# A graph network block on one core: the inverse transform of its convolution as 64-row matmuls on two halves of TensorE's array

## The chip, the cores and the metric

One Trainium2 chip, one NeuronCore of it. The metric is the time of one execution on the device, in microseconds (us). An execution is given by the median of the runs that were timed; a profiled execution has a time of its own, and beside it a span, from its first instruction to its last.

## What is computed

64 graphs of 256 nodes with 256 channels go through two layers, each fed with relu(layernorm(x)) and added to x. Layer 0 is a normalised graph convolution. Layer 1 takes three things from its input h:

```python
xc = transpose(h)                       # channels x nodes
c  = relu(bn(conv1d(xc, w1, 0)))        # 1 tap
c  = bn(conv1d(c, w2, 8))               # 17 taps along the 256 nodes, 256 -> 256 channels
x_conv = transpose(relu(c + xc))
A = exp(-dist(h));  x_nmp = A @ relu(h @ w_msg.T + b_msg)
gi = concat(x_conv, x_nmp) @ w_ih.T + b_ih
gh = h @ w_hh.T + b_hh                  # then the three gates of a GRU cell
out = x + (1 - z) * tanh(gi_n + r * gh_n) + z * h
```

## The kernel before, in words

The convolution with 17 taps is computed by overlap and add in the frequency domain. Each graph's 256 nodes are cut into four tiles of 64, each is transformed with length NT = 80 (80 real rows of spectrum), multiplied bin by bin with the transformed filter, and transformed back. The inverse transform of one graph takes 4 x 80 = 320 rows of spectrum, for 256 output channels, to 256 nodes, tiles overlapping by 16 nodes.

The program has three stages. In the first (0 to 690 us of the profile) a software pipeline goes over the 64 graphs: layer 0, the norms, the one-tap convolution, the messages and the forward transform. In the second (690 to 906 us) TensorE multiplies the spectra of all graphs with the filter, bin by bin, and the products go to a DRAM tensor, `y_d`. In the third (906 to 1789 us) a loop goes over 32 pairs of graphs: inverse transforms, then the matmuls of the gates (`gate`, all recorded on L113, in `multiply`). Most matmuls of this kernel split each number in a high and a low part of type fp32r and take three products; the inverse transform is one plain fp32 matmul per product, and an fp32 matmul leaves two records of LDWEIGHTS and two of MATMUL in the trace.

Around the change:

- `load_y` (L917 to L924), on SyncE's queue, brings the 320 rows of graph b to one of three buffers, `yt`: one DMA for the rows 0 to 127 and 192 to 319 (pieces of 1 KB), one for the rows 128 to 191 on partitions 0 to 63. It waits until the transform of graph b - 3 is done. `y_d` is padded by 64 rows for the first DMA's reading pattern.
- Partitions 64 to 127 of the third block are set to zero once, by three memsets on GpSimd (L1474), so that this block too is a matmul over 128 rows; `idft` waits for them (`yz`).
- `idft` (L1007 to L1022), on TensorE, does per graph and half of the output channels (o) three matmuls: stationary operand 128 rows x 128 channels of `yt`, moving operand 136, 136 and 144 columns of the table `gt`, accumulated in PSUM. Both halves lie in one bank, 4 + b % 2.
- `branch_sum` (L1024, VectorE) adds bias and h to the bank, `branch_scalar` (L1053, ScalarE) and `branch_lo` (L1042, VectorE) make the high and low parts `xcx`, which the gates of the next pair read. 
- The order on TensorE is written out in the loop over the pairs: gates of the first half of the channels (36 matmuls), `idft(b + 2)`, gates of the second half (36 matmuls) with `idft(b + 3)` ahead of the last 18 of them. Only the first pair differs: `idft(0)` and `idft(1)` stand together inside its first gates. There the gate HN of the second half (`hn_bank`, bank 6) is computed ahead of its turn; otherwise HN is in bank 0.

The borders of the blocks are in this line:

```python
BLOCKS = ((0, 128, 0, 136), (192, 320, 120, 256), (128, 192, 56, 200))   # rows from, to; nodes from, to
```

Of the kernel before, what the change touches and what calls it, by code (L numbers as in the profile page):

```python
# [8 lines left out]
F32 = mybir.dt.float32  # L9
F32R = mybir.dt.float32r  # L10
ACT = mybir.ActivationFunctionType
# [3 lines left out]
NT = 80  # L15
# [26 lines left out]

BLOCKS = ((0, 128, 0, 136), (192, 320, 120, 256), (128, 192, 56, 200))


def idft_table():

    g = np.zeros((4 * NT, 4 * TILE + 16))  # L50
    for j in range(4):
        g[j * NT:j * NT + NT, j * TILE:j * TILE + NT] = spectrum_rows(np.arange(NT) - 8, True).T
    out = np.zeros((128, sum(end - first for _, _, first, end in BLOCKS)))
    at = 0
    for top, bottom, first, end in BLOCKS:
        out[0:bottom - top, at:at + end - first] = g[top:bottom, first + 8:end + 8]
        at += end - first
    return out.astype(np.float32)


def tap_table():
# [58 lines left out]
ldx0 ldx1 lda0 lda1 lat0 lat1 st0 ag0a ag0 deg0 degm rs0 dd sd sbias hd ah agg aghi aglo  # L120
out0 u x2 sx20 sx21 st1 ag1a ag1 rs1 n1b xn xnt xt sxt xxhi xxlo s uvf uvh uv cm0 cm1 tcm0 tcm1 h1 mshi mslo
dist af am axhi axlo nmp nm snm dft0 dft1 xe0 xe1 sxa0 sxa1 sxb0 sxb1
unit yz wev wevd lxh0 lxh1 xsum xhi xlo wsum wpart whi0 whi wlo frq com mt ye sy0 sy1 sy2 sy3
lwg0 lwg1 lwg2 lwg3 lwg4 lwg5 wghi wg ly0 ly1 ly2 lxn0 lxn1 lnm0 lnm1 nmhi nmlov nmlop xnhi xnlov xnlop
idf xct xchi xclo ghn gr gin gz gn tr v w nn tz dl e oo lx20 lx21 ot osb so0 so1
""".split()
# [2 lines left out]
def gnn_kernel(nc, x, adj, adjt, w0t, w1mt, wset, wgt, w2r, bc, cols, ftab, gtab, ttab, eye, out):  # L129
    NB = x.shape[0]  # L130
# [12 lines left out]
    xh_d = nc.dram_tensor("xh_d", (128, 2, NF // 2, NG, 64), F32, kind="Internal").ap()  # L143
    xn_d = nc.dram_tensor("xn_d", (NP, 128, 2, 2, 256), F32, kind="Internal").ap()
    x2_v = x2_d.rearrange(blocked, n=2, i=32, h=2, k=32)
    y_all = nc.dram_tensor("y_d", (NB * 4 * NT + 64, 256), F32, kind="Internal").ap()
    y_d = y_all[0:NB * 4 * NT].rearrange("(b r) o -> b r o", b=NB)
    nm_d = nc.dram_tensor("nm_d", (NB, 128, 512), F32, kind="Internal").ap()

    with ExitStack() as ctx:  # L150
        S = {n: ctx.enter_context(nc.semaphore(n)) for n in NAMES}
        P = [ctx.enter_context(nc.psum_tensor(f"P{i}", [128, 512], F32)) for i in range(8)]
# [2 lines left out]
        ident = keep("ident", [128, 128])  # L155
        col = keep("col", [128, 32])
        cold = keep("cold", [128, 24])
        gt = keep("gt", [128, 416])
        bse, low_u, low_v = col[:, 28:29], col[:, 29:30], col[:, 30:31]
        b2, hrz, hn_b, n_b = cold[:, 6:8], cold[:, 8:12], cold[:, 12:14], col[:, 20:22]  # L160
        tt_w = keep("tt_w", [119, 567])
# [69 lines left out]
        yo = [p2(f"yo{i}", [128, 512]) for i in range(4)]  # L231

        xnx.append(p3.hl("xnx1", [128, 2, 512]))
        yt = [p3(f"yt{i}", [128, 3, 256]) for i in range(3)]
        nmx = [p3.hl(f"nmx{i}", [128, 2, 512]) for i in range(2)]
        xct = [p3(f"xct{i}", [128, 2, 256]) for i in range(2)]
        xcx = [p3.hl(f"xcx{i}", [128, 2, 2, 256]) for i in range(2)]
# [679 lines left out]
        def load_y(e, b):  # L917
            e.wait_ge(S["frq"], 2 * NF)
            e.wait_ge(S["idf"], b - 2)
            for n in (b // 32, b // 32 + 2):  # L920
                e.wait_ge(S[f"sy{n}"], 16 * (2 * NF // 4))
            e.e.dma_start(yt[b % 3][:, 0:2, :], y_all[4 * NT * b:4 * NT * b + 384].rearrange(
                "(k p) o -> p k o", p=192)[0:128]).then_inc(S[f"ly{b % 3}"], 16)
            e.e.dma_start(yt[b % 3][0:64, 2, :], y_d[b][128:192]).then_inc(S[f"ly{b % 3}"], 16)  # L924

        def load_pair(e, p):
            e.wait_ge(S["whi"], 30)
# [73 lines left out]
            e.e.tensor_tensor(o[1][:, :, :], xnf[p % 2][:, :, :, :].rearrange("p c i t -> p c (i t)"),  # L1001
                              o[0][:, :, :], ALU.subtract).then_inc(done, 1)

        def idft_bank(b):
            return 4 + b % 2

        def idft(e, b):  # L1007
            k = idft_bank(b)
            e.wait_ge(S[f"ly{b % 3}"], 2 * loaded(b, 3))
            e.wait_ge(S["gt_in"], 16)  # L1010
            e.wait_ge(S["yz"], 1)
            e.wait_ge(S["xct"], b - 1)
            y = yt[b % 3]
            for o in range(2):


                g = 0
                for j, (_, _, first, end) in enumerate(BLOCKS):
                    t = e.e.matmul(P[k][:, o * 256 + first:o * 256 + end], y[:, j, o * 128:o * 128 + 128],  # L1019
                                   gt[:, g:g + end - first], start=o == 0 and j == 0, stop=j == 2, skip_group_check=True)  # L1020
                    g += end - first
            t.then_inc(S["idf"], 1)  # L1022

        def branch_sum(e, b):  # L1024
            p, n = b // 2, b % 2
            t = xct[b % 2]
            e.wait_ge(S["idf"], b + 1)
            e.wait_ge(S[f"lxn{p % 2}"], loaded(p, 2))
            e.wait_ge(S["xclo"], b - 1)
            e.wait_ge(S["xchi"], b - 1)  # L1030
            for c in range(2):
                d = e.e.scalar_tensor_tensor(out=t[:, c, :], in0=P[idft_bank(b)][:, c * 256:c * 256 + 256],
                                             scalar=b2[:, c:c + 1], in1=xnf[p % 2][:, c, n, :],
                                             op0=ALU.add, op1=ALU.add)
            d.then_inc(S["xct"], 1)
# [19 lines left out]

        HN, R, IN, Z = 0, 1, 2, 3
        LAST_Z = (Z, HN)

        def hn_bank(n):

            return 6 if n == 1 else HN

        def gate(e, p, o, k, n, blocks, first, last, at=0, end=512):
            xc = [h[:, :, :, :].rearrange("p c i t -> p c (i t)") for h in xcx[p % 2]]
# [6 lines left out]
        def gates_tensor(e, p, o, middle, late):  # L1071
            n = 2 * p + o
            e.wait_ge(S["xnhi"], p + 1)
            e.wait_ge(S["xnlov"], 1)
            e.wait_ge(S["xnlop"], p)
            e.wait_ge(S["wg"], 2)
            e.wait_ge(S["ye"], 2 * NF - 1)
            e.wait_ge(S["gn"], n)
            if n != 1:
                gate(e, p, o, HN, 2, [4, 5], True, True).then_inc(S["ghn"], 1)  # L1080
            e.wait_ge(S["ye"], 2 * NF)
            e.wait_ge(S["tr"], n)
            gate(e, p, o, R, 0, [4, 5], True, False)
            if n == 0:
                gate(e, p, o, Z, 1, [4, 5], True, False)
            e.wait_ge(S["wg"], 4)
            e.wait_ge(S["nmhi"], 2 * p + 2)
            e.wait_ge(S["nmlov"], 2)
            e.wait_ge(S["nmlop"], 2 * p)
            gate(e, p, o, R, 0, [2, 3], False, False)  # L1090
            if n == 0:
                gate(e, p, o, Z, 1, [2, 3], False, False)
                middle()
                gate(e, p, o, IN, 2, [2, 3], True, False)
                gate(e, p, 1, hn_bank(1), 2, [4, 5], True, True).then_inc(S["ghn"], 1)
            e.wait_ge(S["wg"], 6)
            e.wait_ge(S["xchi"], 2 * p + 2)
            e.wait_ge(S["xclo"], 2 * p + 2)
            gate(e, p, o, R, 0, [0, 1], False, True).then_inc(S["gr"], 1)
            if n == 0:  # L1100
                gate(e, p, o, IN, 2, [0, 1], False, True).then_inc(S["gin"], 1)
                gate(e, p, o, Z, 1, [0, 1], False, True).then_inc(S["gz"], 1)
                return
            e.wait_ge(S["w"], n)
            gate(e, p, o, IN, 2, [2, 3, 0, 1], True, True).then_inc(S["gin"], 1)
            late()
            e.wait_ge(S["tz"], n)
            if n == 2 * NP - 1:

                e.wait_ge(S["gn"], 2 * NP)  # L1110
                for i, k in enumerate(LAST_Z):
                    gate(e, p, o, k, 1, [4, 5, 2, 3, 0, 1], True, True, 256 * i, 256 * i + 256).then_inc(S["gz"], 1)
                return
            gate(e, p, o, Z, 1, [4, 5, 2, 3, 0, 1], True, True).then_inc(S["gz"], 1)

        def gates_scalar(e, p, o, middle, late):
            n = 2 * p + o
            e.wait_ge(S["ghn"], n + 1)
            e.wait_ge(S["nn"], n)
            e.e.activation(gn[:, :], P[hn_bank(n)][:, :], ACT.Identity, scale=0.5, bias=hn_b[:, o:o + 1]).then_inc(S["gn"], 1)  # L1120
            middle()
            e.wait_ge(S["gr"], n + 1)
            e.wait_ge(S["e"], n)
            e.e.activation(tr[:, :], P[R][:, :], ACT.Tanh, scale=0.5, bias=hrz[:, o:o + 1]).then_inc(S["tr"], 1)  # L1124
            e.wait_ge(S["w"], n + 1)
            e.wait_ge(S["oo"], n)
            e.e.activation(nn[:, :], gn[:, :], ACT.Tanh, bias=n_b[:, o:o + 1]).then_inc(S["nn"], 1)  # L1127
            late()
            if n == 2 * NP - 1:
                e.wait_ge(S["oo"], n)  # L1130
                for i, k in enumerate(LAST_Z):
                    e.wait_ge(S["gz"], n + 1 + i)
                    e.e.activation(tz[:, 256 * i:256 * i + 256], P[k][:, 0:256], ACT.Tanh, scale=0.5,
                                   bias=hrz[:, 2 + o:3 + o]).then_inc(S["tz"], 1)
                return
            e.wait_ge(S["gz"], n + 1)
            e.wait_ge(S["oo"], n)
            e.e.activation(tz[:, :], P[Z][:, :], ACT.Tanh, scale=0.5, bias=hrz[:, 2 + o:3 + o]).then_inc(S["tz"], 1)  # L1138
# [303 lines left out]
        def _(gpsimd):  # L1442
# [27 lines left out]
                spectra_lo(e, f)  # L1470
            e.wait_ge(S["xlo"], NF)
            e.wait_ge(S["frq"], 2 * NF)
            for t in yt:
                d = gpsimd.memset(t[64:128, 2, :], 0.0)  # L1474
            d.then_inc(S["yz"], 1)
            e.wait_ge(S["yz"], 1)
            for p in range(NP - 1):
                split_xn_lo(e, p + 1, S["xnlop"])
                split_nm_lo(e, 2 * p + 2, S["nmlop"])
# [86 lines left out]
```

## Time and profile before

| | us |
|---|---|
| median of 3 runs (1788.72 to 1789.57) | 1789.55 |
| the profiled execution | 1790.36 |
| its span | 1788.6 |
| PE, matmuls, busy | 1774.4 (99%) |
| PEld, weight loads, busy | 1574.9 (88%) |
| DVE (VectorE) busy | 1212.5 (68%) |
| ACT (ScalarE) busy | 997.3 (56%) |
| POOL (GpSimd) busy | 830.7 (46%) |

PE is TensorE with its matmuls and PEld the same engine with its weight loads, which overlap the matmuls. Matmuls are pipelined and their recorded ends are modelled, so the duration of one record is longer than the step from one to the next; the chain of waits gives the steps.

### The profile page before, as it was taken

What the parts mean: (1) busy time and instruction counts of PE and PEld (TensorE: products, weight loads), DVE (VectorE), ACT (ScalarE), POOL (GpSimd) and SP (SyncE); (2) the same over time, 40 slices, a digit from 0 to 9 for tenths busy, and PEclk for the clock granted to TensorE, in tenths of its full rate; (3) what the DMA queues carried; (4) which work ended last, traced back from release to release, by engine and by line L of the source; (5) the groups of instructions that cost most, each with busy time, mean ns of one, the idle gap of its engine ahead of it and who ended that gap; (6) DMA issues with size and microseconds to landing.
All of it is one profiled execution on the core that took longest, in us unless ns stands there. A gap on an engine that the chain in (4) does not pass through costs nothing.

```text
span 1788.6 us, 29955 instructions
## 1 busy us (share of the span) xinstructions
PE 1774.4 (99%) x10266; PEld 1574.9 (88%) x10266; DVE 1212.5 (68%) x2318; ACT 997.3 (56%) x1787; POOL 830.7 (46%) x991
## 2 busy tenths in 40 slices
PE   8999999999999999999999999999999999999998
PEld 7999999999999999999988888888888888888887
DVE  8999999999999847665664454554554544545545
ACT  5888888888888876665743233233332332332322
POOL 5788888887777627655722122221221221212211
PEclk9999999999999999999999999999999999999999
DMA  6566666676656554544762534534435345344342
GB/s 214 179 201 210 206 207 209 201 214 191 209 184 202 144 163 148 179 161 171 245 189 73 123 79 108 116 78 116 93 97 120 79 107 116 81 115 101 91 111 42
DMA packets 511381, 262.56 MB, mean 147 GB/s; under 512 B 366215, under 2 KB 474119, under 8 KB 511230
## 3 DMA queue, kind: packets, MB, share of 16 engines
q1 hardware_dynamic: 510686, 260.58, 52.3%
q8 instruction: 83, 1.36, 0.3%
q14 instruction: 68, 0.56, 0.1%
q10 hardware_dynamic: 544, 0.07, 0.0%
HBM read 151.51 MB, written 109.05 MB: 146 GB/s over the span
## 4 chain that ended last, share of the span: by engine, by line
PE 97%; issue 1%; POOL 1%; DVE 0%; ACT 0%; DMA 0%; SPq 0%; POOLq 0%; ACTq 0%; DVEq 0%
PE P L113 72%; PE P L615 6%; PE P L1019 5%; PE P L874 4%; PE P L644 4%; PE P L706 3%; PE P L663 1%; PE P L624 1%; PE P L1488 1%; DMA tt_w<-in_ttab 0%; POOL axl L578 0%; POOL af L575 0%; ACT xn L354 0%; DVE wh0l L837 0%; DVE x L473 0%
## 5 line engine op out<-in xcount | busy, mean ns | idle before, releaser
L1001 POOL TENSOR_TENSOR xnx1l<-xnf,xnx1h 128x1024 fp32r<-128x1024 f32 x16 | 44.2, 2761 | 336.2 <-ACT xnx1h L994 336.2
L1001 POOL TENSOR_TENSOR xnx0l<-xnf,xnx0h 128x1024 fp32r<-128x1024 f32 x15 | 41.6, 2774 | 317.1 <-ACT xnx0h L994 317.1
L1124 ACT ACTIVATE tr<-P,cold 128x512 f32<-128x512 f32 x64 | 44.2, 690 | 192.3 <-PE P L113 192.3
L1127 ACT ACTIVATE nn<-gn,col 128x512 f32<-128x512 f32 x64 | 46.4, 724 | 182.3 <-DVE gn L1148 182.3
L1157 DVE SCALAR_TENSOR_TENSOR tz<-tz,tr 128x512 f32<-128x512 f32 x63 | 43.6, 692 | 142.5 <-ACT tz L1138 142.5
L1138 ACT ACTIVATE tz<-P,cold 128x512 f32<-128x512 f32 x63 | 43.4, 688 | 156.8 <-PE P L113 156.8
L1144 DVE SCALAR_TENSOR_TENSOR gn<-tr,gn 128x512 f32<-128x512 f32 x64 | 45.0, 703 | 125.9 <-ACT tr L1124 125.9
L575 POOL TENSOR_TENSOR af<-af,at 128x512 f32<-128x512 f32 x64 | 110.1, 1720 | 42.8 <-ACT af L366 40.5
L578 POOL TENSOR_TENSOR axl<-af,axh 128x512 fp32r<-128x512 f32 x64 | 101.2, 1582 | 55.6 <-ACT axh L384 55.6
L615 PE MATMUL P<-ah,hd 128*128 128x256 f32 x512 | 121.4, 380 | 0.0
L113 PE MATMUL P<-w1mh,xxh 128*128 128x512 f32 x256 | 107.9, 422 | 0.0
L1019 PEld LDWEIGHTS P<-gt,yt 128*128 128x128 f32 x768 | 98.9, 190 | 4.9
L615 PEld LDWEIGHTS P<-ah,hd 128*128 128x128 f32 x512 | 93.2, 191 | 10.0
L113 PE MATMUL P<-w1mh,xxl 128*128 128x512 f32 x256 | 101.2, 395 | 0.0
L113 PE MATMUL P<-w1ml,xxh 128*128 128x512 f32 x256 | 101.1, 395 | 0.0
L1019 PE MATMUL P<-gt,yt 128*128 128x136 f32 (+1 forms) x768 | 100.8, 281 | 0.0
L498 DVE SCALAR_TENSOR_TENSOR x<-x,x 128x512 f32<-128x512 f32 x64 | 99.8, 1559 | 0.1
L899 DVE TENSOR_TENSOR yo<-P,mt 128x512 f32<-128x512 f32 x78 | 53.5, 686 | 66.5 <-PE P L113 66.5
L1148 DVE TENSOR_TENSOR gn<-gn,P 128x512 f32<-128x512 f32 x64 | 44.0, 688 | 66.9 <-PE P L113 66.9
L706 PE MATMUL P<-tt_w,taps 119*128 119x140 f32 (+1 forms) x592 | 80.8, 283 | 0.0
L113 PE MATMUL P<-w0h,agh 128*128 128x256 f32 x256 | 77.5, 303 | 3.2 <-DVE w0l L463 2.1
L726 ACT COPY wf<-P 128x420 f32<-128x420 f32 (+1 forms) x94 | 46.8, 512 | 60.1 <-PE P L706 59.9
(215 smaller groups left out, 6423.0 us busy)
## 6 DMA issues: line engine op xcount, KB each, us to landing
xh_d<-xst SPq DMA_DIRECT2D x64, 320.0 KB, 4.6
y_d<-yo SPq DMA_DIRECT2D x80, 256.0 KB, 2.2
xl<-xh_d SPq DMA_DIRECT2D x36, 512.0 KB, 4.5
x<-in_x SPq DMA_DIRECT2D x64, 256.0 KB, 2.7
a<-in_adj SPq DMA_DIRECT2D x64, 256.0 KB, 3.1
at<-in_adjt SPq DMA_DIRECT2D x64, 256.0 KB, 3.9
x_d<-x SPq DMA_DIRECT2D x64, 256.0 KB, 4.2
xn_d<-xt SPq DMA_DIRECT2D x64, 256.0 KB, 4.0
```

The source lines that it names most:

```text
L113: done = e.matmul(o, l, r, start=start, stop=stop, skip_group_check=True)
L498: e.e.scalar_tensor_tensor(out=o[:, :, :], in0=o[:, :, :], scalar=0.0, in1=xs[b % 5][:, :, :], op0=ALU.max, op1=ALU.add).then_inc(S["x2"], 1)
L575: e.e.tensor_tensor(af[:, :], af[:, :], at[b % 7][:, :], ALU.mult).then_inc(S["am"], 1)
L578: e.e.tensor_tensor(ax[1][:, :], af[:, :], ax[0][:, :], ALU.subtract).then_inc(S["axlo"], 1)
L615: t = e.e.matmul(P[AG][:, f * 256:f * 256 + 256], hd[b % 2][:, m, f * 128:f * 128 + 128], ah[b % 2][:, m * 256:m * 256 + 256], start=m == ...
L644: t = e.e.matmul(P[k][:, n * 2 * NT:n * 2 * NT + 2 * NT], h1[b % 2][:, n, c * 128:c * 128 + 128], ft[:, :], start=True, stop=True, skip_gr ...
L706: t = e.e.matmul(P[k][:, m * 140:m * 140 + 140], taps[0:n_rows, j0 + m, c * 128:c * 128 + 128], tt_w[0:n_rows, part * 140:part * 140 + 140 ...
L726: e.e.copy(dst, src).then_inc(S["wev"], 1)
L874: t = e.e.matmul(common(chunk)[:, 0:256], xsum[f % 3][:, c, 128 * chunk:128 * chunk + 128], wsum[f % 3][:, c, :], start=c == 0, stop=c == ...
L899: e.e.tensor_tensor(yo[n % 4][:, :].rearrange("p (q o) -> p q o", q=2), main(chunk)[:, :].rearrange("p (q o) -> p q o", q=2), mt[chunk][:, ...
L1001: e.e.tensor_tensor(o[1][:, :, :], xnf[p % 2][:, :, :, :].rearrange("p c i t -> p c (i t)"), o[0][:, :, :], ALU.subtract).then_inc(done, 1)
L1019: t = e.e.matmul(P[k][:, o * 256 + first:o * 256 + end], y[:, j, o * 128:o * 128 + 128], gt[:, g:g + end - first], start=o == 0 and j == 0 ...
```

## The change

The 320 rows of a graph are cut into five blocks of 64 rows. Each block reaches the nodes of REACHED. The half o of the output channels uses partitions 64 o to 64 o + 63 for its spectrum and for a copy of the table, and accumulates in a bank of its own, 4 + 2 (b % 2) + o. The matmuls of the two halves alternate. The table grows from 416 to 560 columns, the buffers `yt` from 3 x 256 to 5 x 128 numbers per partition, the memsets and the padding go, and HN always uses bank 0, so that the early HN of the first pair waits for ScalarE to have read the bank (`gn`).

```diff
-BLOCKS = ((0, 128, 0, 136), (192, 320, 120, 256), (128, 192, 56, 200))
+REACHED = ((0, 72), (0, 136), (56, 200), (120, 256), (184, 256))
+GT_COLUMNS = sum(end - first for first, end in REACHED)
...
+    out = np.concatenate([g[64 * q:64 * q + 64, first + 8:end + 8] for q, (first, end) in enumerate(REACHED)], axis=1)
+    return np.concatenate([out, out]).astype(np.float32)
...
-        yt = [p3(f"yt{i}", [128, 3, 256]) for i in range(3)]
+        yt = [p3(f"yt{i}", [128, 5, 128]) for i in range(3)]
...
-            e.e.dma_start(yt[b % 3][:, 0:2, :], y_all[4 * NT * b:4 * NT * b + 384].rearrange(
-                "(k p) o -> p k o", p=192)[0:128]).then_inc(S[f"ly{b % 3}"], 16)
-            e.e.dma_start(yt[b % 3][0:64, 2, :], y_d[b][128:192]).then_inc(S[f"ly{b % 3}"], 16)
+            for o in range(2):
+                e.e.dma_start(yt[b % 3][64 * o:64 * o + 64, :, :], y_d[b].rearrange("(q p) o -> p q o", p=64)[
+                    :, :, 128 * o:128 * o + 128]).then_inc(S[f"ly{b % 3}"], 16)
...
-        def idft_bank(b):
-            return 4 + b % 2
+        def idft_bank(b, o):
+            return 4 + 2 * (b % 2) + o
...
-            e.wait_ge(S["yz"], 1)
...
-            for o in range(2):
-                g = 0
-                for j, (_, _, first, end) in enumerate(BLOCKS):
-                    t = e.e.matmul(P[k][:, o * 256 + first:o * 256 + end], y[:, j, o * 128:o * 128 + 128],
-                                   gt[:, g:g + end - first], start=o == 0 and j == 0, stop=j == 2, skip_group_check=True)
-                    g += end - first
+            g = 0
+            for q, (first, end) in enumerate(REACHED):
+                for o in range(2):
+                    rows = slice(64 * o, 64 * o + 64)
+                    t = e.e.matmul(P[idft_bank(b, o)][:, first:end], y[rows, q, :], gt[rows, g:g + end - first],
+                                   start=q == 0, stop=q == 4, skip_group_check=True)
+                g += end - first
...
-                gate(e, p, 1, hn_bank(1), 2, [4, 5], True, True).then_inc(S["ghn"], 1)
+                e.wait_ge(S["gn"], 1)
+                gate(e, p, 1, HN, 2, [4, 5], True, True).then_inc(S["ghn"], 1)
...
-            for t in yt:
-                d = gpsimd.memset(t[64:128, 2, :], 0.0)
-            d.then_inc(S["yz"], 1)
-            e.wait_ge(S["yz"], 1)
...
-    nc = bacc.Bacc("TRN2", target_bir_lowering=False, num_devices=1)
+    nc = bacc.Bacc("TRN2", target_bir_lowering=False, num_devices=1, dynamic_dma_scratch_size=8192)
```

## Rows read from the trace of the kernel before

**Rows 1.** The stages: busy time of each engine in three stretches
```profile
core 0: us, PE busy (x) PEld busy (x) DVE busy (x) ACT busy (x) POOL busy (x), PEclk, DMA share, GB/s
0.00:690.00 690.00, 681.08 (x4456) 626.51 (x4457) 635.01 (x1509) 582.15 (x1142) 503.17 (x825) 1.00 0.63 193
690.00:906.00 216.00, 216.00 (x1571) 208.08 (x1570) 134.84 (x159) 135.37 (x228) 135.41 (x71) 1.00 0.56 191
906.00:1788.60 882.60, 877.35 (x4242) 740.33 (x4240) 442.66 (x651) 279.81 (x418) 192.09 (x96) 1.00 0.44 100
```

**Rows 2.** The page's chain that ended last, by line
```profile
PE P L113 72%; PE P L615 6%; PE P L1019 5%; PE P L874 4%; PE P L644 4%; PE P L706 3%; PE P L663 1%; PE P L624 1%; PE P L1488 1%; DMA tt_w<-in_ttab 0%; POOL axl L578 0%; POOL af L575 0%; ACT xn L354 0%; DVE wh0l L837 0%; DVE x L473 0%
```

**Rows 3.** The chain of waits, 1160 to 1210 us: start, us, what
```profile
1167.79 1.42 PE P L1019 x12
1169.21 8.21 PE P L113 x36
1177.42 1.42 PE P L1019 x12
1178.83 16.37 PE P L113 x72
```

**Rows 4.** Groups of instructions by line and form: busy us, mean ns
```profile
L1019 PE MATMUL P<-gt,yt 128*128 128x136 f32 x512 | 80.1, 279 | 0.0
...
L1019 PE MATMUL P<-gt,yt 128*128 128x144 f32 x256 | 52.4, 286 | 0.0
...
L1019 PEld LDWEIGHTS P<-gt,yt 128*128 128x128 f32 x768 | 98.9, 190 | 4.9
```

**Rows 5.** The timeline around one transform: start, us, what
```profile
1204.44 0.39 PE L113 MATMUL P<-xcx0h,wgl 128*128 128x512 f32 x1
1204.44 1.59 PEld L1019 LDWEIGHTS P<-gt,yt 128*128 128x128 f32 x12
1204.67 1.58 PE L1019 MATMUL P<-gt,yt 128*128 128x136 f32 x12
...
1205.99 0.49 PE L113 MATMUL P<-xnx0h,wgh 128*128 128x512 f32 x1
```

**Rows 6.** Four transposes on PE's timeline, and their group by form
```profile
505.23 0.60 PE L663 MATMUL P<-ident,xn 128*128 128x128 f32 x4
...
L663 PE MATMUL P<-ident,xn 128*128 128x128 f32 x256 | 38.4, 273 | 0.9 <-ACT xn L354 0.9
```

**Rows 7.** PE's timeline, first stage: a product over 96 rows between others
```profile
499.97 0.60 PE L615 MATMUL P<-ah,hd 128*128 128x256 f32 x2
500.22 0.59 PE L624 MATMUL P<-uv 96*128 96x256 f32 x2
500.64 0.28 PE L113 MATMUL P<-xxh,wseh 128*128 128x256 f32 x1
```

**Rows 8.** Groups by form, second stage: the filter's transform
```profile
L706 PE MATMUL P<-tt_w,taps 119*128 119x140 f32 x372 | 52.3, 283 | 0.0
...
L706 PE MATMUL P<-tt_w,taps 68*128 68x140 f32 x12 | 2.4, 283 | 0.0
```

**Rows 9.** Timelines of ACT, DVE and PE in the first pair
```profile
908.46 0.68 ACT L1120 ACTIVATE gn<-P,cold 128x512 f32<-128x512 f32 x1
...
916.43 1.48 DVE L1042 SCALAR_TENSOR_TENSOR xcx0l<-xct,xcx0h 128x512 fp32r<-128x512 f32 x2
...
916.81 0.39 PE L113 MATMUL P<-xnx0h,wgh 128*128 128x512 f32 x1
...
918.18 0.40 PE L113 MATMUL P<-xcx0h,wgh 128*128 128x512 f32 x1
```

**Rows 10.** The instructions on the tile yt, and their landings
```profile
L922 SPq DMA_DIRECT2D yt<-y_d x64: 371/502/1418, 907.1 to 1732.5; - x64
L924 SPq DMA_DIRECT2D yt<-y_d x64: 472/483/1473, 907.5 to 1733.0; - x64
L1474 POOL MEMSET yt<- x3: 311/311/313, 906.0 to 906.5; 64x256 f32 x3
...
DMA to landing us min/median/max: 2.4/3.7/6.0
```

**Rows 11.** Timeline of SyncE's queue, and the chain, around one load
```profile
922.20 0.59 SPq L922 DMA_DIRECT2D yt<-y_d x1
...
948.48 1.42 PE P L1019 x12
```

More of the change, by code:

```diff
@@ L52, in idft_table @@
         g[j * NT:j * NT + NT, j * TILE:j * TILE + NT] = spectrum_rows(np.arange(NT) - 8, True).T
[L53 to L58, printed above, removed]
+    out = np.concatenate([g[64 * q:64 * q + 64, first + 8:end + 8] for q, (first, end) in enumerate(REACHED)], axis=1)
+    return np.concatenate([out, out]).astype(np.float32)
 def tap_table():
@@ L122 @@
 dist af am axhi axlo nmp nm snm dft0 dft1 xe0 xe1 sxa0 sxa1 sxb0 sxb1
-unit yz wev wevd lxh0 lxh1 xsum xhi xlo wsum wpart whi0 whi wlo frq com mt ye sy0 sy1 sy2 sy3
+unit wev wevd lxh0 lxh1 xsum xhi xlo wsum wpart whi0 whi wlo frq com mt ye sy0 sy1 sy2 sy3
 lwg0 lwg1 lwg2 lwg3 lwg4 lwg5 wghi wg ly0 ly1 ly2 lxn0 lxn1 lnm0 lnm1 nmhi nmlov nmlop xnhi xnlov xnlop
@@ L145, in gnn_kernel @@
     x2_v = x2_d.rearrange(blocked, n=2, i=32, h=2, k=32)
-    y_all = nc.dram_tensor("y_d", (NB * 4 * NT + 64, 256), F32, kind="Internal").ap()
-    y_d = y_all[0:NB * 4 * NT].rearrange("(b r) o -> b r o", b=NB)
+    y_d = nc.dram_tensor("y_d", (NB, 4 * NT, 256), F32, kind="Internal").ap()
     nm_d = nc.dram_tensor("nm_d", (NB, 128, 512), F32, kind="Internal").ap()
@@ L157, in gnn_kernel @@
         cold = keep("cold", [128, 24])
-        gt = keep("gt", [128, 416])
+        gt = keep("gt", [128, GT_COLUMNS])
         bse, low_u, low_v = col[:, 28:29], col[:, 29:30], col[:, 30:31]
@@ L1002, in split_xn_lo @@
                               o[0][:, :, :], ALU.subtract).then_inc(done, 1)
-        def idft_bank(b):
-            return 4 + b % 2
+        def idft_bank(b, o):
+            return 4 + 2 * (b % 2) + o
         def idft(e, b):
-            k = idft_bank(b)
             e.wait_ge(S[f"ly{b % 3}"], 2 * loaded(b, 3))
             e.wait_ge(S["gt_in"], 16)
-            e.wait_ge(S["yz"], 1)
             e.wait_ge(S["xct"], b - 1)
             y = yt[b % 3]
-            for o in range(2):
-                g = 0
-                for j, (_, _, first, end) in enumerate(BLOCKS):
-                    t = e.e.matmul(P[k][:, o * 256 + first:o * 256 + end], y[:, j, o * 128:o * 128 + 128],
-                                   gt[:, g:g + end - first], start=o == 0 and j == 0, stop=j == 2, skip_group_check=True)
-                    g += end - first
+            g = 0
[5 more added lines that the diff above has]
+                g += end - first
             t.then_inc(S["idf"], 1)
@@ L1031, in branch_sum @@
             for c in range(2):
-                d = e.e.scalar_tensor_tensor(out=t[:, c, :], in0=P[idft_bank(b)][:, c * 256:c * 256 + 256],
+                d = e.e.scalar_tensor_tensor(out=t[:, c, :], in0=P[idft_bank(b, c)][:, 0:256],
                                              scalar=b2[:, c:c + 1], in1=xnf[p % 2][:, c, n, :],
@@ L1057, in gnn_kernel @@
         LAST_Z = (Z, HN)
-        def hn_bank(n):
-            return 6 if n == 1 else HN
         def gate(e, p, o, k, n, blocks, first, last, at=0, end=512):
@@ L1119, in gates_scalar @@
             e.wait_ge(S["nn"], n)
-            e.e.activation(gn[:, :], P[hn_bank(n)][:, :], ACT.Identity, scale=0.5, bias=hn_b[:, o:o + 1]).then_inc(S["gn"], 1)
+            e.e.activation(gn[:, :], P[HN][:, :], ACT.Identity, scale=0.5, bias=hn_b[:, o:o + 1]).then_inc(S["gn"], 1)
             middle()
```

## The prediction

> **What bounds the kernel now.** I read the stages first: TensorE is busy for 877 of the 883 us of the third stage, at a granted clock of 1.00 (the 2.4 GHz level), while VectorE is busy for half of it and ScalarE for a third [rows 1]. The chain that ended last says the same: nearly all of it is PE, and 5% of the span is L1019, the inverse transform [rows 2]. The chain of waits in one pair gives its price: one transform takes 1.42 us, and the next gates begin where it ends, with no piece between [rows 3]. So what the change does to the 64 transforms on TensorE goes to the end one for one: 64 x 1.42 = 90.9 us, which agrees with the 5%. All else counts only if it comes late.
>
> Inside a transform there are 12 records (6 fp32 matmuls, two records each), of 136 and 144 columns [rows 4]. 2 x (136 + 136 + 144) x 2 records = 1664 columns in 1.42 us is 0.85 ns per column. The weight loads last 0.19 us each, yet 12 of them lie side by side in 1.59 us and start ahead of their matmuls [rows 4, 5]: they are hidden now. TensorE is bound by columns here, and the change cuts the columns but adds records: 5 blocks x 2 halves x 2 records = 20 loads and 20 matmuls, of 72, 136, 144, 136 and 72 columns: 560 x 2 x 2 = 2240 columns. Only if the two halves of the array stream at the same time does this fall to the worth of 1120.
>
> **The sum, part by part.**
>
> *Columns and loads.* A record of 72 columns would stream in 72 x 0.85 = 0.061 us, but its next weights must come too. What is the shortest step that a load allows? Nothing in the trace has fewer than 128 columns on both sides; four transposes of 128 columns take 0.60 us from the first's start to the last's end, and one record lasts 0.273 [rows 6]: (0.60 - 0.273) / 3 = 0.109 per step. 128 columns at 0.85 are also 0.109, so this row bounds the floor from above and does not show it: 0.109 at most, 0.061 at least. I take 0.109, because it is the nearest row with a load per record, and keep 0.061 as the other end.
>
> *Overlap.* Matmuls run in program order. In the new order (two records of half 0, two of half 1, and again) the second record of half 0 can run beside the first of half 1, the second of half 1 beside the first of the next block. That gives 11 slots for 20 records: with 0.109 for the 4 slots that hold 72 columns alone, 0.116 for the 4 whose longer record has 136, 0.123 for the 3 with 144, 0.436 + 0.464 + 0.369 = 1.27 us. With 0.061 in the 4 short slots it is 1.08. Against 1.42 that is -0.15 (to -0.34) per transform, 64 x = **-9.6 us** (to -21.8). No row of this trace shows two matmuls at once, so the other end is none of it: 8 x 0.109 + 8 x 0.116 + 4 x 0.123 = 2.29 us, +55.7 us in all.
>
> *Switching the array's division.* Each visit to the transform now goes from instructions over all rows to instructions over half of them, and back: 63 visits (graphs 0 and 1 share one), 126 switches. Lower bound 0: a product over 96 rows between 128-row ones ends 0.24 us after its predecessor for two matmuls (500.57 to 500.81), no more than the 0.12 steps around it [rows 7]; a group over 68 rows has the duration of one over 119 [rows 8]; and the change from fp32 to fp32r behind a transform costs nothing either (1206.25 to 1206.48, the usual 0.23) [rows 5]. A gain is excluded, since a step can't end before its columns are in. But none of these rows divides the array in two that work apart. If the array must be empty before it is divided anew, a switch costs the tail that is hidden now: the 12 records reach over 1.58 us while TensorE moves on by 1.42 [rows 3, 5], so 0.16. If the first load behind the switch can't be hidden either, 0.16 + 0.19 = 0.35 [rows 4]. I take 0.16: nearer to what a division must do than the rows with 0, which change only how many rows of one array are filled. 126 x 0.16 = **+20.2 us** (0 to +44).
>
> The Trainium skill speaks against the change here: "TensorEngine Tiling (Array Packing)", Key Properties, states that changing the tiling mode drains TensorE, while tiles within a mode run loads and matmuls in parallel. It gives no price: by it the sum is that of the emptied array, 1800, and not that of the rows with 0, 1780, and the overlap is real. No run here shows either half yet.
>
> *The wait for `gn` in the first pair.* ScalarE ends `gn` at 909.14; the early HN gate begins at 916.81 [rows 9]. 7.7 us of slack, cost nothing; it would take a ScalarE that is late by that much. Behind the waiting HN stand the last gates of the pair, which wait for `xcx`'s low parts (916.43 + 1.48 = 917.91) and begin at 918.18 [rows 9]. This chain hangs on the end of the second transform and moves with it; once, at most some tenths of a us.
>
> *Loads of the spectrum.* Two DMAs per graph before and after, the same 320 KB, but 640 pieces of 512 B in place of 320 of 1 KB. Issue on SyncE's queue is some 0.5 us each, landing 3.7 us in the median [rows 10]. The load issued at 922.20 is for the transform at 948.48 [rows 11]: 26 us. Even a landing twice as long is hidden, and DMA is at 0.44 of its time [rows 1]. Cost nothing; if the cover went, it would be a wait of TensorE ahead of L1019.
>
> *Memsets, table, banks, DMA scratch.* Three memsets (0.31 us each on GpSimd, at 906 [rows 10]) go: they end 6 us before the first transform. The table is loaded once, in the first stage. VectorE reads two banks in place of one, with as many instructions. No DMA is issued from GpSimd. All nothing.
>
> **Sum**: -9.6 + 20.2 = +10.6 us. Against the profiled execution's own 1790.36 that is 1801.0; the median of the runs stands 0.8 below it, so the forecast for the median is 1800.
>
> **Rivals.** (B) *Overlap without a price of switching*, the other side: the rows with 96 and 68 rows and the type change all switch for nothing [rows 5, 7, 8]. Then -9.6 to -21.8 us: **1768 to 1780**. It decides as soon as a switch costs less than 0.076 us (9.6 / 126). Against it: those rows keep one array.
> (C) *The matmuls overlap, the loads don't.* 20 loads one behind the other at 0.109 are 2.18 us, +0.76, +48.6 us: **1838**, with switches 1858. For it: the 12 loads of a transform start one per step, never two together [rows 5]. Against it: each of them fills all rows, so they could not do otherwise.
> (D) *The change doesn't do what it says*: the halves run one after the other, 2.29 us, +55.7: **1845**, with switches 1865. For it: no row shows two matmuls at once. By the Trainium skill's section neither C nor D should happen.
>
> **Chances.** Forecast (overlap, switches cost 0.08 to 0.35, -1.6 to +34.5 us, 1788 to 1824) 0.41; B 0.34; C 0.11; D 0.14. The range has to leave out at most 0.2: from B's low end, 1768, to just over C's, 1842; D and the dear half of C are outside. The likeliest case's own range is 1788 to 1824. 0.2% (3.6 us) is about what a measurement of this kernel can tell from no change. Faster: B and a little of the forecast's low end, 0.36; same 0.09; slower 0.55.
>
> **What would show it.** In the chain of waits after, one transform (x20) takes 1.4 to 1.6 us if the forecast holds, with two records of L1019 starting within some 10 ns of each other, steps of 0.11 to 0.12 per pair, and a stop of about 0.16 us ahead of the first record and behind the last. B: 1.1 to 1.27 us and gates that follow at once. C: pairs of matmuls start together but only each 0.22 us. D: 20 starts, each 0.11 or more apart, 2.3 us. It would be wrong altogether if TensorE waited for `yt`, or if the clock fell from 1.00 in the third stage as half of the array idles; then the gates' step of 0.23 would grow as well.

## The result, and the profile after

The changed kernel takes 1794.45 us (median of 9 runs, 1794.24 to 1795.23) against 1789.55 us: ratio 1.0029, 95% interval 1.0018 to 1.0039. It is slower by 4.9 us. The forecast was 10.6 us slower: the side was right, the size twice too large.

The third stage is longer by as much, and nothing else moved. These are the stages after, same columns as [rows 1]:

```profile
0.00:690.00 690.00, 680.93 (x4459) 625.31 (x4460) 634.76 (x1510) 582.55 (x1142) 503.93 (x825) 1.00 0.64 193
690.00:906.00 216.00, 216.00 (x1571) 207.91 (x1570) 134.02 (x159) 135.55 (x228) 135.35 (x71) 1.00 0.55 191
906.00:1793.40 887.40, 882.29 (x4753) 723.01 (x4751) 442.58 (x651) 279.29 (x418) 191.45 (x93) 1.00 0.43 99
```

TensorE is busy for 882.3 of 887.4 us, before 877.4 of 882.6; the clock is still 1.00. 887.4 - 882.6 = 4.8 us is the whole difference of the spans (1793.4 against 1788.6).

The chain of waits of the kernel after, the same stretch as [rows 3] (start, us, what):

```profile
1168.91 1.31 PE P L1016 x20
1170.22 8.41 PE P L111 x36
1178.62 1.31 PE P L1016 x20
1179.93 16.57 PE P L111 x72
```

A transform (L1016 now) went from 1.42 to 1.31 us: less, with 20 records in place of 12. But the gates behind it, which the change does not touch, went from 8.21 to 8.41 and from 16.37 to 16.57. Per pair: -0.22 + 0.40 = +0.18 us; from start to start a pair went from 27.42 to 27.59 us, +0.17. Times 31 pairs that is 5.3 us, near the 4.9 measured. (A pair has 36 + 72 = 108 gate matmuls, so each half of the channels has 54 and not 36, as the text on the kernel before has it: 36 is what stands between the two transforms of a pair.)

Where these 0.20 us lie is seen on the timeline, which answers to [rows 5]:

```profile
1205.82 0.39 PE L111 MATMUL P<-xcx0h,wgl 128*128 128x512 f32 x1
1206.14 1.23 PEld L1016 LDWEIGHTS P<-gt,yt 64*128 64x128 f32 x20 [0.35 <-issue]
1206.14 1.38 PE L1016 MATMUL P<-gt,yt 64*128 64x72 f32 x20
...
1207.45 0.19 PEld L111 LDWEIGHTS P<-xnx0h,wgh 128*128 128x128 f32 x1
1207.45 0.50 PE L111 MATMUL P<-xnx0h,wgh 128*128 128x512 f32 x1
```

Before, the transform's first weight load started at the same time as the last gate matmul (both 1204.44) and lay beside it. Now it starts 0.32 us behind that matmul's start (1205.82 to 1206.14): here the load of the half array did not go ahead of a matmul on the whole array. On the way out it is the same: the first load of the gates starts at 1207.45, 0.20 us after the start of the transform's last matmul (1207.246), which has only 72 columns. That is the stop at each switch, and the page shows it nowhere as idle time of PE, because the modelled ends of the records cover it.

The starts of the first and the last single records of this transform, from the trace, with records between them left out at the dots and at the end of the loads:

```
load    1206.139 1206.146 | 1206.248 1206.254 | 1206.357 1206.364 | 1206.469 1206.475 | ...
matmul  1206.141 1206.148 | 1206.308 1206.314 | 1206.419 1206.426 | ... | 1207.177 1207.184 | 1207.239 1207.246
```

Records come in pairs, 6 or 7 ns apart, the loads too: the two halves of the array do load and multiply at the same time. Rivals C (loads one behind the other) and D (no overlap at all) are out.

### The profile page after: what moved, and what is told of

It reads as the page before. It is cut to its first block, busy times and chain, and to the rows that moved or that the text cites. A ratio compares the mean times of both kernels' runs of the same rounds, so it can differ in the third digit from the quotient of the medians.

```text
span 1793.4 us, 30974 instructions
## 1 busy us (share of the span) xinstructions
PE 1779.2 (99%) x10778; PEld 1556.2 (87%) x10778; DVE 1211.4 (68%) x2318; ACT 997.4 (56%) x1787; POOL 830.7 (46%) x988
## 4 chain that ended last, share of the span: by engine, by line
PE 97%; issue 1%; DVE 1%; POOL 1%; ACT 0%; DMA 0%; SPq 0%; POOLq 0%; ACTq 0%
PE P L111 73%; PE P L612 6%; PE P L1016 5%; PE P L871 4%; PE P L641 4%; PE P L703 4%; PE P L660 1%; PE P L621 1%; DMA st_w<-in_w0t 0%; POOL axl L575 0%; POOL af L572 0%; DVE agl L417 0%; DVE sm L515 0%; ACT agh L358 0%; ACT xn L351 0%
## 5 line engine op out<-in xcount | busy, mean ns | idle before, releaser
L1016 PEld LDWEIGHTS P<-gt,yt 64*128 64x128 f32 x1280 | 78.8, 187 | 22.2 <-issue 22.2
L1016 PE MATMUL P<-gt,yt 64*128 64x72 f32 (+2 forms) x1280 | 87.9, 281 | 0.0
```

Of the source, the lines that this page charges most:

```text
L1016: t = e.e.matmul(P[idft_bank(b, o)][:, first:end], y[rows, q, :], gt[rows, g:g + end - first], start=q == 0, stop=q == 4, skip_group_check ...
```

## The experiments

All are measured against the kernel before, run beside them on the same chip. Where a time is set against the changed kernel, the two medians come from different chips; the kernel before took 1789.55 to 1789.74 us on all of them. In the cuts from the changes, "..." stands for lines left out.

### Fewer visits: both transforms of a pair at one place

```diff
                 if more:
                     idft(e, b + 2)
-                gates_tensor(e, p, 1, lambda: None, lambda: idft(e, b + 3) if more else None)
+                    idft(e, b + 3)
+                gates_tensor(e, p, 1, lambda: None, lambda: None)
```

> The changed kernel with both transforms of a pair at one place: 32 visits to the half-array matmuls in place of 63. Theory (each switch of the array's division stops TensorE for 0.20 us, 0.40 per visit): 31 x 0.40 = 12.4 us less than the changed kernel's 1794.5, 1782, which is also faster than the kernel before. Rival (the loss lies in each transform, whatever stands around it): 1794 to 1795.

Measured: 1787.65 us (11 runs), ratio to the kernel before 0.9989 (0.9981 to 0.9998): 6.8 us less than the changed kernel, not 12.4. The chain of waits in the middle of the stage:

```profile
1170.30 2.46 PE P L1016 x40
1172.77 24.70 PE P L111 x108
1197.47 2.46 PE P L1016 x40
```

A pair now takes 27.17 us against 27.59: one visit fewer saves 0.42. That is 13 us over 31 pairs, so some 6 us were lost elsewhere. TensorE's waits name one part, a single wait in the first pair:

```profile
PE P L1016 <- DMA yt<-y_d: 3.5, 1, 3.5
```

The transform of graph 3 had moved ahead of its load, whose issue stood on SyncE's queue behind the sixteen loads of the residual (`x2l`) and three more. The granted clock shows a second part (columns as in [rows 1]; the third number from the right is the clock):

```profile
918.00:922.00 4.00, 4.00 (x22) 3.06 (x20) 1.38 (x2) 1.32 (x2) 0.00 (x0) 1.00 0.79 155
923.00:926.00 3.00, 0.19 (x6) 0.04 (x2) 2.02 (x4) 2.18 (x4) 1.14 (x1) 1.00 1.14 319
928.00:931.00 3.00, 3.00 (x11) 2.29 (x10) 1.40 (x2) 0.00 (x0) 2.58 (x2) 0.50 0.15 27
932.00:940.00 8.00, 8.00 (x37) 6.64 (x36) 3.24 (x6) 2.05 (x3) 0.00 (x0) 1.00 0.19 49
```

Just behind the wait, from 928 to 931 us, the clock is 0.50 (the 1.2 GHz level), and the gates start 0.43 us apart (929.28, 929.71) in place of 0.23. Summed over the starts, this cost about 1.5 us. With the wait of 3.5 us that is 5 of the 6.

> The kernel before with the same move of the second transform, as a control: no switches there, so 1789.5, no change. If the place of the transforms had a price or a gain of its own, it would show here.

The same edit of the kernel before: 1790.47 us (11 runs), ratio 1.0006 (0.9997 to 1.0015), with the same one wait (3.2 us) and, in the profiled execution, the lower clock behind it (0.50 from 926 to 932 us). That execution took 1793.32 us, the longest of the 11, which go down to 1788.74. So in time this control shows no price of the place, but only because a small gain that I had not expected stands against the wait:

```profile
1172.64 2.83 PE P L1019 x24
1175.47 24.49 PE P L113 x108
1199.97 2.83 PE P L1019 x24
```

27.32 us per pair against 27.42 [rows 3]: one visit fewer gains 0.09 even on the whole array. The change of type as such does not show in the starts: in the kernel before, the second gate matmul starts 0.354 us after the transform's last one (1205.960 to 1206.314), where the columns of the two ask for 0.35. What is longer is a few steps behind each transform: the next nine gates are together some 0.04 us late there, and 0.01 here (medians over the stage). Why is not shown.

### More visits: each transform cut in two

```diff
...
-                for o in range(2):
+                for o in range(2) if q in part else ():
...
-                gates_tensor(e, p, 0, lambda: None if b else (idft(e, 0), idft(e, 1)), lambda: None)
+                gates_tensor(e, p, 0, lambda: None if b else (idft(e, 0), idft(e, 1)),
+                             lambda: idft(e, b + 2, range(2)) if more else None)
                 if more:
-                    idft(e, b + 2)
-                gates_tensor(e, p, 1, lambda: None, lambda: idft(e, b + 3) if more else None)
+                    idft(e, b + 2, range(2, 5) if p else range(5))
+                gates_tensor(e, p, 1, lambda: None, lambda: idft(e, b + 3, range(2, 5)) if more else None,
+                             lambda: idft(e, b + 3, range(2)) if more else None)
```

> The changed kernel with each transform cut in two, blocks 0 and 1 ahead of 18 gate matmuls, blocks 2 to 4 behind them: 124 visits in place of 63. Theory (0.40 us per visit): +24.4 us, 1819. Rival (no price per visit): 1794 to 1796.

Measured: 1820.05 us (4 runs), ratio 1.0168 (1.0153 to 1.0184). 25.6 us over the changed kernel for 61 visits more: 0.42 us per visit, as with fewer visits. The same blocks, the same loads; only the number of times that the array is divided changed, and with it the places between the gates.

```profile
1172.48 0.66 PE P L1016 x8
1173.14 4.31 PE P L111 x18
1177.45 0.85 PE P L1016 x12
```

18 gate matmuls take 4.31 us here; at the pure step of 24.49 / 108 = 0.227 they would take 4.08.

### Is it two halves at work, or any matmul over half of the array?

```diff
-                    t = e.e.matmul(P[k][:, o * 256 + first:o * 256 + end], y[:, j, o * 128:o * 128 + 128],
-                                   gt[:, g:g + end - first], start=o == 0 and j == 0, stop=j == 2, skip_group_check=True)
+                    t = e.e.matmul(P[k][:, o * 256 + first:o * 256 + end], y[0:64 if j == 2 else 128, j, o * 128:o * 128 + 128],
+                                   gt[0:64 if j == 2 else 128, g:g + end - first], start=o == 0 and j == 0, stop=j == 2, skip_group_check=True)
```

> The kernel before with its third block over 64 rows (partitions 0 to 63) in place of 128 rows of which 64 are zero: the same columns, loads and records, but 4 switches per transform, no partner on the other half. Theory (any matmul over half of the array costs 0.20 us on the way in and on the way out): 256 x 0.20 = +51 us, 1841. Rival (the price comes from two halves at work, or only rows at partition 64 and up divide the array): 1789.5, no change.

Measured: 1838.18 us (4 runs), ratio 1.0273 (1.0259 to 1.0287), 48.6 us over the kernel before.

```profile
1182.15 2.00 PE P L1019 x12
1184.15 8.38 PE P L113 x36
```

The same 12 records take 2.00 us in place of 1.42, and the gates behind them 8.38 in place of 8.21. 48.6 / 256 switches is 0.19 each. It needs neither a second half at work nor rows at partition 64 and up: both forms of the rival are out. This is the price that the zero rows of the third block avoid in the kernel before.

### Is the overlap what shortens the transform?

```diff
-            g = 0
-            for q, (first, end) in enumerate(REACHED):
-                for o in range(2):
+            for o in range(2):
+                g = 0
+                for q, (first, end) in enumerate(REACHED):
                     rows = slice(64 * o, 64 * o + 64)
...
-                g += end - first
+                    g += end - first
```

> The changed kernel with the loops over the halves and the blocks exchanged: all 10 records of half 0, then all 10 of half 1, same banks, same instructions. Theory (the gain inside a transform is two halves at work at once, and that needs neighbours in program order on different halves): a transform takes about 20 steps of 0.11 = 2.2 us in place of 1.1, +70 us, 1865. Rival (TensorE finds the pairs itself by looking ahead): 1794 to 1800.

Measured: 1844.33 us (4 runs), ratio 1.0304 (1.029 to 1.0319). 49.9 us over the changed kernel, not 70.

```profile
1183.11 2.11 PE P L1016 x19
1185.22 8.38 PE P L111 x36
```

2.11 us in place of 1.31: with one half after the other the gain turns into a loss, so the theory stands. But 2.2 us and a stop of 0.2 were to be expected. From first to last start each half takes 1.098 us (1183.042 to 1184.140, 1183.852 to 1184.950), just as long as the two side by side in the changed kernel (1206.141 to 1207.239). What is missing from twice that is an overlap of 0.29 us at the seam. The trace has the starts

```
half 0, matmuls 7 to 10:  1183.846  1183.962  1184.078  1184.140
half 1, matmuls 1 to 4:   1183.852  1184.019  1184.130  1184.295
```

(the column counts 136, 136, 72, 72 and 72, 72, 136, 136 tell them apart; a "matmul" here is one record). The first matmul of half 1 is the 11th of the program and starts ahead of the 8th.

### What bounds a transform now?

```diff
-REACHED = ((0, 72), (0, 136), (56, 200), (120, 256), (184, 256))
+REACHED = ((0, 128), (0, 136), (56, 200), (120, 256), (128, 256))
```

> The changed kernel with the first and last block's moving operand widened from 72 to 128 columns (the added columns of the table are zeros). Theory (a transform is 10 pairs of weight loads at 0.109 us each, and the 72-column matmuls hide behind them): 2 x (0.109 + 0.116 + 0.123 + 0.116 + 0.109) = 1.15 us in place of 1.11, +2 to +3 us, 1797. Rival (bound by columns): 112 columns x 2 records at 0.85 ns = 0.19 us per transform, +12 us, 1807.

Measured: 1797.77 us (5 runs), ratio 1.0045 (1.0032 to 1.0059), 3.3 us over the changed kernel for 20% more columns.

```profile
1179.13 1.35 PE P L1016 x20
```

1.35 in place of 1.31 us. Most of the columns that were saved in the 72-column blocks lie in the shade of the weight loads: 10 pairs of loads, 0.109 us apart in the changed kernel where they set the pace (1206.139, .248, .357 above), while 72 columns ask for 0.061.

### A version that is faster than both

```diff
             for b in range(3):
                 load_y(e, b)
-            for p in range(2):
-                load_x2(e, p)
+            load_x2(e, 0)
+            load_y(e, 3)
+            load_x2(e, 1)
...
-                    if p == 0:
-                        load_y(e, 3)
```

on top of the move of the transforms, once on the changed kernel and once on the kernel before.

> The changed kernel with both transforms of a pair at one place, and the load of graph 3's spectrum issued ahead of the second half of the residual's first loads. The grouped kernel waited once, 3.5 us, for that load. Theory (31 fewer visits save about 0.42 us each, as the period of a pair fell from 27.59 to 27.17 us, and the one wait hid a part of it): 3.5 us less than the grouped kernel's 1787.7, 1784. Rival (the loads behind it come too late instead, and another wait takes its place): 1787 to 1788.

Measured: 1782.30 us (5 runs), ratio to the kernel before 0.9958 (0.9945 to 0.997). The wait for `yt` is gone from TensorE's waits, and the first pairs run through:

```profile
912.55 2.46 PE P L1016 x40
915.01 7.02 PE P L111 x30
922.04 2.46 PE P L1016 x40
924.50 10.65 PE P L111 x46
```

It gained 5.4 us, not 3.5: with the wait, the stretch at the lower clock behind it went too (the granted clock is 1.00 there now), which had cost about 1.5 us. The other 0.4 us is not accounted for. Over the changed kernel the gain is 12.2 us for 31 visits fewer, 0.39 each.

> The kernel before with the same two moves, as the control. Its period of a pair was 27.32 us grouped against 27.17 of the changed kernel. Theory: 31 x 0.15 = 4.6 us over the changed kernel with these moves, 1787 to 1789. Rival (the half-array matmuls bring nothing once the wait is gone): the same time as the other.

Measured: 1786.98 us (11 runs), ratio 0.9985 (0.9976 to 0.9994). Like for like, with half as many visits, the half-array transform is 4.7 us faster than the one on the whole array; with one visit per transform it is 4.9 us slower.

## Why the prediction was half right

- **What bounds, and that nothing else counts: right.** TensorE's chain carries all of the 4.8 us. The memsets, the table and the wait for `gn` left no trace. The loads land after 4.3 us in place of 3.7 and are waited for only in the grouped experiments, where I had moved a transform ahead of its load.
- **Overlap: real, as forecast, but the term was mis-sized; this is the step that failed.** I made the transform 1.27 us, -0.15, -9.6 us in all. Without its switch it is 1.13 us: a pair of 27.59 us less 24.49 for the gates less 2 x 0.42 for the visits leaves 2 x 1.13. That is -0.29 per transform, -18.6 us. Two things in the sum were too dear. I took the program's order as the order of starts and got 11 slots; the halves start together and there are 10, which at the same prices make 1.15. And I put 0.109 on each short slot, where the last step of a transform is 0.062 (1207.177 to 1207.239): its load was already done ahead. The floor of 0.109 itself is right where loads follow loads (1206.139, .248, .357 with 72 columns).
- **Switching: that each switch stops TensorE was right, the price too low.** I took 0.16 us, the hidden tail of the pipeline, as a guess at its cause, which no run shows by itself. Three runs with 32, 124 and (on the other kernel) 128 visits give 0.42, 0.42 and 0.38 per visit, 0.19 to 0.21 per switch: +26.5 us for 63 visits and not +20.2. A visit on the whole array, which I called free, costs 0.09: 2.8 us over 31 pairs. It falls away as the other comes, since the price per visit includes it.
- **The sum.** Measured terms: -0.29 x 2 + 0.42 x 2 - 0.09 = +0.17 us per pair, 5.3 us over 31 pairs, against 4.9 measured. My errors, -9 us on the overlap, +6 us on the switches and -3 us on the visit that I took as free, cancelled in part: that the forecast was off by only 6 us is in part luck.
- **How firm the split is.** It takes a visit to cost the same wherever it stands. The starts alone give another one. A transform, from its first start to its last and the columns of the last record, takes 1.17 us against 1.41: -0.25, -15.9 us in all. Around it the gap to the first record is 0.318 us against 0.228, and the second gate starts 0.25 us later than the columns ask for: +0.335 per visit, +21.1 us. By this reading the switches were priced nearly right; the overlap is the term that was off by either.
- **The sign that I named** was a transform of 1.4 to 1.6 us in the chain, 1.1 to 1.27 for B. It was 1.31, which fits neither: the slots were ten and not eleven, and the chain puts the stop on the way out to the gates.
- **The range of the likeliest case** does not follow from its condition: switches of 0.08 us with the smaller overlap give +0.5 us, with the larger one -11.7, and not -1.6.
- **Rivals.** B (no price of switching) would have needed under 0.076 us per switch, or with the overlap as it was measured 0.15 (18.6 / 126); it is 0.2. Its rows [rows 7, 8] are true, but they have 96 and 68 rows, and the runs show the price for 64. C and D are out by the pairs of starts.
- **The rule that I drew on.** The Trainium skill, "TensorEngine Tiling (Array Packing)", Key Properties, states that a change of the tiling mode drains TensorE, and that tiles load and multiply in parallel. These traces agree with both: 0.2 us per switch, and loads 6 to 7 ns apart. That the stop is a drain they do not show by themselves.

Open: whether each half needs a bank of its own for this was not tried. Nor did a run take the 0.2 us apart. The run over 64 rows alone shows where it lies: into the third block the load starts 0.09 us later than the 136 columns before it ask for (1182.335 to 1182.543), and the second record comes 0.10 us later than 144 columns ask for (1182.544 to 1182.771).

## What to carry to other kernels

In this kernel two matmuls over 64 rows each on different halves of the array ran at once, fp32 with their weight loads too (starts 6 to 7 ns apart), when they were neighbours in the program; but each further visit from whole-array matmuls and back cost about 0.4 us. So count visits before columns: gather the half-array work of several items in one place, and pad a lone 64-row block to more rows rather than switch for it (here 48.6 us). When work is moved ahead on one engine, move its load ahead on the queue as well: a wait of 3.5 us cost TensorE a stretch at the lower clock on top (about 1.5 us).

## What the runs showed of the hardware that I had not expected

- The two halves do not keep one order of starts between them: in the run with the halves in turn, the 11th matmul of the program started ahead of the 8th, 0.29 us ahead of the 10th. Within a half the order held. The prediction's sentence that matmuls run in program order does not hold between the halves.
- A matmul over 64 rows alone, on partitions 0 to 63, costs two switches, 0.19 us each, with nothing on the other half; the products over 68 rows at L706 show no such thing: their starts, and those behind them, keep steps of 0.12 us in the kernel before (661.282, 661.401, 661.525, 661.642).
- One visit fewer to the fp32 matmuls gained 0.09 us on the whole array as well (27.42 against 27.32 us per pair). The cause is open.
- A single wait of TensorE, of 3.5 and 3.2 us in the two grouped runs, was followed by a granted clock of 0.50 (the 1.2 GHz level): from 928 to 931 us in one, from 926 to 932 in the other. It came back to 1.00 with the matmuls running on. The same kernels without the wait stay at 1.00.
